# A graph network's pair loop: per-chunk target windows in steps of 64, and zero multiplies between the stages

## The chip, the core and the metric

The program runs on one core of one Trainium2 chip, in one launch. The metric is device time in microseconds, from the first to the last instruction and what the runtime puts around them; lower is better. A core has the engines TensorE (in the profile PE for its matmuls, PEld for its weight loads), VectorE (DVE), ScalarE (ACT), GpSimd (POOL) and SyncE (SP, here only DMA issues). [...]

## What is computed

One pass of four graph layers over 1024 nodes of 128 features, with 16384 edges sorted by target. Cut to what matters:

```python
# L0: a message per edge, summed by source node
m = concat([x[row], x[col]]); m = relu(relu(m @ Wm1 + bm1) @ Wm2 + bm2)
m_sum = segment_sum(m, row, 1024)
h = relu(relu(concat([x, m_sum, match(x)]) @ Wn1 + bn1) @ Wn2 + bn2)
# L1: three attention layers over the same edges, with a layer norm between them
# L2: mean over neighbours, then W;   L3: sum of neighbours weighted by edge_weight, then an MLP
```

Each layer is entered through a layer norm (ln0, ln1, ln4, ln5), and ln2 and ln3 stand between the attention layers. L1 needs how many edges lead from each node to each other, L2 whether there are any (with repeats kept up to a cap), L3 the sum of their weights. The kernel makes these as dense 1024 x 1024 matrices (counts and weights), while it computes L0's messages.

## The kernel before

**Sort.** The edges are sorted by the block of 128 nodes that their source lies in (`src >> 7`), stable, so within a block they keep the order of their targets. They are laid out in pairs of two chunks, 128 edges each (`PAIR` is 256); each block is padded to whole pairs. There are eight blocks and, with these inputs, 68 pairs. `dstf` holds each slot's target, `valid` says whether a slot is filled, one column a chunk.

**Pair loop.** For each block, a loop over its pairs `g` on four engines at once. TensorE multiplies one-hots: `OHc` (sources, with a rank cap) and `OHe` (sources times each of three parts of the edge's weight) against `OHd`, a chunk's one-hots of its targets, 1024 wide. The results add up in PSUM: banks 0 and 1 hold the block's 128 x 1024 counts, banks 2 and 3 the weights. Not all of the 1024 targets are gone over: `rngi` holds one packed number for each pair, the span, with the first block of 128 targets that the pair touches and the last one, and TensorE loads it into a register (L1230). A dynamic loop over the span (L1237), here called a pass, does two blocks of 128 targets at once, for both chunks: 16 matmuls.

The order of a pair on TensorE: ranks (L1176), load the span (L1230), source parts of the message of pair g + 2 (L1185), passes (L1242 counts, L1245 weights), message sums (L1251), ranks for the next pair (L1176), transposes and the two layers of the next pair's messages (L1163, L1170, L1171). Between engines it goes by semaphores:
- VectorE makes the next `OHd` (L928) when TensorE's first L1251 has signalled `counts_added`. Behind it come the rank products (L903), which signal `ranks_read`.
- TensorE's `ranks` of the pair wait for `ranks_read`, and all that follows on its sequencer stands behind that wait.
- ScalarE makes `OHe` (L546), `OHs32` (L548), and the activations (L557, L560). VectorE adds biases (L914) and messages (L888). GpSimd gathers table rows (L399) and turns sources into one-hots (L413).

**Setup of the spans.** VectorE marks for all chunks and all eight blocks of targets which slots lie in it (`inblk`, L826), TensorE sums the marks over the edges (L1195), and VectorE makes the first and last block of each pair from them (L849, L857, then the short operations from L861 to L876). The messages of the first two pairs (L860, L895) stand among these on VectorE.

**The normalisations.** For ln1 to ln5 VectorE makes mean and variance (L711, L712), ScalarE the root (L472, signals `ln_sd`), VectorE the scales and half of the rows (L725), ScalarE the others where it is shared. TensorE has nothing to do until the first rows are there. Its first work then is: ln1 eight transposes (L1075) and the rows of the attention (L1328); ln2 and ln3 transposes (L1321) and L1328; ln4 the means (L1436); ln5 the weighed sums (L1464).

The places that the change touches:

## Time and profile before

| | us |
|---|---|
| median of 3 runs | 999.43 |
| lowest, highest | 998.51, 1005.07 |
| the profiled execution, its own time | 995.34 |
| its span, first to last instruction | 993.5 |
| mean granted clock of TensorE | 0.962 |

The span is what the profile's rows add up to; 1.8 us lie around it. Rows give start and duration in microseconds from the span's start, or a count and nanoseconds of one. "Idle before" in brackets says how long an engine was idle ahead of a group and what released it; "issue" is time in which it waited for nothing that the profile shows. [...]

### The profile page before, as it was taken

How to read it: one execution, taken by the hardware profiler on the slowest of the kernel's cores; microseconds unless marked ns; L12 is line 12 of the kernel's file. 1: busy time of each engine (PE TensorE's matmuls, PEld its weight loads, DVE VectorE, ACT ScalarE, POOL GpSimd, SP SyncE). 2: the span in 40 equal slices, each digit the busy share in tenths (PEclk: the TensorE clock that was granted, in tenths of full speed). 3: DMA queues.
4: the chain of work that ended last, by engine and by line, in shares of the span. 5: the costliest groups of instructions: out<-in, count | busy, mean ns of one | idle time of the engine just before them, and what ended most of it. 6: DMA issues, size and time to landing. Idle time of an engine off the chain costs nothing.

```text
span 993.5 us, 18362 instructions
## 1 busy us (share of the span) xinstructions
PE 876.5 (88%) x5355; PEld 545.8 (55%) x5356; DVE 666.2 (67%) x1778; ACT 502.4 (51%) x1006; POOL 291.9 (29%) x424
## 2 busy tenths in 40 slices
PE   3999958999899999999999998689978996899668
PEld 1556736878787878787878745322232222322134
DVE  6399985666666666666666763577757784967650
ACT  6232104555555556555555564466645674566521
POOL 5030036545444545454544400011132110121000
PEclk9999987999999999999999999799979998999979
DMA  3020032111111111111112300000000000000300
GB/s 80 28 81 1 1 115 66 42 63 51 60 49 59 48 63 47 59 50 56 53 55 47 68 1 1 1 0 1 1 1 0 1 1 0 1 1 0 132 38 21
DMA packets 19144, 35.85 MB, mean 36 GB/s; under 512 B 5280, under 2 KB 11552, under 8 KB 18976
## 3 DMA queue, kind: packets, MB, share of 16 engines
q0 software_dynamic: 7104, 19.41, 6.9%
q1 hardware_dynamic: 12000, 15.95, 4.8%
q8 instruction: 20, 0.33, 0.1%
q14 instruction: 20, 0.16, 0.1%
HBM read 29.56 MB, written 5.79 MB: 36 GB/s over the span
## 4 chain that ended last, share of the span: by engine, by line
PE 75%; DVE 13%; ACT 6%; issue 3%; DMA 1%; POOL 1%; DVEq 0%; ACTq 0%; POOLq 0%
PE PS L1374 9%; PE PS L1251 7%; PE PS L1245 6%; PE PS L1170 5%; PE PS L1359 5%; PE PS L1171 5%; PE PS L1185 5%; PE PS L1120 4%; PE PS L1365 4%; PE PS L1328 3%; PE PS L1242 3%; PE PS L1292 3%; DVE OHd L986 3%; PE PS L1163 3%; PE PS L1176 2%
## 5 line engine op out<-in xcount | busy, mean ns | idle before, releaser
L399 POOL DMA_INDIRECT BT<-Qtab,gidx x148 | 149.9, 1013 | 96.3 <-DVE gidx L813 61.2
L546 ACT ACTIVATE OHe<-OHs,sew 128x128 bf16<-128x128 bf16 x408 | 126.6, 390 | 63.5 <-PE PS L1251 63.0
L986 DVE CUSTOM_DVE_ANT_0 OHd<-PS,n1T 128x1024 bf16<-128x1024 f32 x96 | 112.1, 1220 | 19.5 <-PE PS L1328 19.5
L413 POOL TENSOR_SCALAR KV<-BT,pid 128x256 bf16<-128x256 uint8 x74 | 69.9, 945 | 176.2 <-DVE MS L888 170.8
L557 ACT ACTIVATE m2s<-m2s 128x512 f32<-128x512 f32 x68 | 42.8, 630 | 108.4 <-DVE m2s L914 108.4
L928 DVE TENSOR_SCALAR OHd<-iotaN,dstf 128x1024 bf16<-128x1024 f16 x136 | 64.0, 509 | 37.6 <-PE PS L1251 37.5
L1170 PE MATMUL PS<-Wm,m1T 128*128 128x256 f32 x276 | 83.2, 383 | 0.0
L914 DVE TENSOR_TENSOR m2s<-PS,bm 128x512 f32<-128x512 f32 x68 | 47.0, 691 | 53.6 <-PE PS L1171 53.6
L1171 PE MATMUL PS<-Wm,m1T 128*128 128x256 f32 x276 | 82.6, 381 | 0.0
L452 POOL TENSOR_TENSOR zl<-AL,Sx 128x8 f32<-128x8 f32 x12 | 2.6, 216 | 265.1 <-DVE Sx L986 265.1
L1251 PE MATMUL PS<-OHs,m2s 128*128 128x128 f32 x544 | 79.9, 291 | 0.0
L1245 PE MATMUL PS<-OHd,OHe 128*128 x852 | 78.0, 225 | 0.0
L1120 PE MATMUL PS<-KV,m2s 128*128 128x288 f32 x256 | 72.6, 429 | 2.8 <-DVE KV L805 2.6
L1185 PE MATMUL PS<-SKT,KV 128*128 (+1 forms) x420 | 61.0, 282 | 14.5 <-issue 7.4
L888 DVE TENSOR_TENSOR MS<-PS,BT 128x512 f32<-128x512 f32 x68 | 47.0, 692 | 36.8 <-PE PS L1185 36.8
L1251 PEld LDWEIGHTS PS<-OHs,m2s 128*128 128x128 f32 x544 | 67.8, 196 | 6.4
L1242 PE MATMUL PS<-OHd,OHc 128*128 x284 | 64.2, 226 | 3.2 <-issue 0.6
L1365 PE MATMUL PS<-rowA,sel 128*128 128x512 bf16 x192 | 57.8, 382 | 10.4 <-ACT rowA L645 8.6
L805 DVE SCALAR_TENSOR_TENSOR KV<-iota,hi,carried 128x288 f32<-128x288 f32 x128 | 65.8, 514 | 0.0
L1120 PEld LDWEIGHTS PS<-KV,m2s 128*128 128x128 f32 x256 | 46.0, 195 | 27.3 <-DVE KV L805 14.5
L997 DVE SCALAR_TENSOR_TENSOR PS<-msum,s,BT 128x1024 f32<-128x1024 f32 x30 | 38.8, 1293 | 30.8 <-ACT Wn L654 24.1
L1245 PEld LDWEIGHTS PS<-OHd,OHe 128*128 128x128 bf16 x852 | 56.3, 100 | 4.3
(349 smaller groups left out, 1704.2 us busy)
## 6 DMA issues: line engine op xcount, KB each, us to landing
BT<-Wtab SPq DMA_DIRECT2D x1, 4096.0 KB, 12.8
BT<-Qtab,gidx POOLq DMA_INDIRECT x148, 2.8
BT<-Stab SPq DMA_DIRECT2D x1, 2048.0 KB, 10.2
Wtab<-H SPq DMA_DIRECT2D x4, 512.0 KB, 2.8
Wtab<-cs SPq DMA_DIRECT2D x4, 512.0 KB, 2.9
Qtab<-BT SPq DMA_DIRECT2D x1, 1024.0 KB, 4.5
Wn<-in_L_gnn_Wn SPq DMA_DIRECT2D x1, 1024.0 KB, 5.5
x<-in_x SPq DMA_DIRECT2D x1, 512.0 KB, 4.2
```

What stands on the lines that cost most here:

```text
L399: g.indirect_dma_start(out=G[:, p % SLOTS, k, :], out_offset=None, in_=Qtab, in_offset=bass.IndirectOffsetOnAxis(ap=gidx[:, p, k:k + 1], a ...
L546: a.activation(OHe[:, k, j, :], OHs[:, k, :], ACT.Copy, scale=sew[:, j, bass.ds(2 * g + k, 1)])
L986: v.tensor_tensor_reduce(junk[n % 2], bank(4, 2), mask[:, i, :], 1.0, 2 * FAR, ALU.subtract, ALU.max, Sx[:, i, hd:hd + 1]).then_inc(S("gat ...
L1120: t.matmul(bank(5)[:, 0:2 * NCH], OHlo[:, i % RING, :], KV[:, i % RING, :, :].rearrange("p k c -> p (k c)"), start=(i == 0), stop=(i == T ...
L1170: t.matmul(to, m1T[:, k, :], Wm2[:, 0, :], start=True, stop=False)
L1171: return t.matmul(to, m1T[:, 2 + k, :], Wm2[:, 1, :], start=False, stop=True)
L1185: last = t.matmul(bank(5)[:, k * F2:(k + 1) * F2], OHsT[:, slot, k * P:(k + 1) * P], Pp[:, blk, j, :], start=(j == 0), stop=(j == 2))
L1242: t.matmul(PS[:, bass.ds(at, P)], OHc[:, k, :], dst, start=False, stop=False, skip_group_check=True)
L1245: t.matmul(PS[:, bass.ds(at + 2 * BANK, P)], OHe[:, k, j, :], dst, start=False, stop=False, skip_group_check=True)
L1251: last = t.matmul(bank(4)[:, f * P:(f + 1) * P], m2s[:, k, f * P:(f + 1) * P], OHs32[:, k, :], start=False, stop=False, skip_group_check=True)
L1365: last = t.matmul(tile(hd, j)[:, half * BANK:(half + 1) * BANK], sel[:, half, :], rowA[:, hd % 2, :], start=False, stop=False, skip_group_ ...
L1374: last = t.matmul(bank(6 + hd % 2)[half * P // 2:half * P // 2 + C + 1, :], HX[:, j, hd, :], EC[n % 4][:, half * BANK:(half + 1) * BANK], ...
```

## The change

Each chunk gets a window of its own, 128 targets wide, that starts at a multiple of 64. The packed span holds the first unit of 64 targets of both chunks, how far the loop goes, and the block of the sources. A pass now does one window for each chunk: 8 matmuls. If a chunk touches three or more units, or starts in the last unit of a PSUM bank, both chunks of the pair start at an even unit and the pair takes as many passes as are needed. The ends of each chunk's targets come from transposing `dstf` and `rngp` and reducing over the edges, and the packed number is worked out in one row. Also, TensorE multiplies zeros (`steady`) while the normalisations run: a number of 128x512 multiplies ahead of the wait for `ln_sd`, some behind it, and five behind the transposes.

```diff
@@ -37,6 +37,8 @@
 FRAC = 1.0 / 1024.0
 FAR = -1e30
 BANK = 512
+UNITS = 15 << 6
+WFIRST, WCOUNT, WBLK = 1 << 6, 1 << 10, 1 << 14
 
 fp32, bf16, fp16 = mybir.dt.float32, mybir.dt.bfloat16, mybir.dt.float16
 i32, u32, i16, u8 = mybir.dt.int32, mybir.dt.uint32, mybir.dt.int16, mybir.dt.uint8
@@ -386,7 +387,7 @@
                 split(g.tensor_scalar(pblk[:, 1, :], iota[0:FEW, 0:NPAIR], pb[0:FEW, b:b + 1], None, ALU.is_ge))
                 split(g.tensor_tensor(pblk[:, 0, :], pblk[:, 0, :], pblk[:, 1, :], ALU.add))
             split(g.tensor_copy(pblki[:], pblk[:, 0, 1:2]))
-            g.tensor_scalar(pblk[:, 1, 0:NPAIR - 2], pblk[:, 0, 2:NPAIR], float(NB * NB), None, ALU.mult)
+            g.tensor_scalar(pblk[:, 1, 0:NPAIR - 2], pblk[:, 0, 2:NPAIR], float(WBLK), None, ALU.mult)
             g.memset(pblk[:, 1, NPAIR - 2:NPAIR], 0.0).then_inc(S("pair_blocks"), 1)
             eng.wait_ge(S("tables_stored"), 16)
             eng.wait_ge(S("indices_ready"), 1)
@@ -819,13 +819,9 @@
             link(v.tensor_copy(srcl[:], ssrc[:]))
             link(v.scalar_tensor_tensor(srcl[:], srcl[:], 1.0, valid[:], ALU.add, ALU.mult))
             v.tensor_scalar(srcl[:], srcl[:], -1.0, None, ALU.add).then_inc(S("sources_ready"), 1)
-            v.tensor_copy(paired(dstf), sdst)
-            link(v.tensor_scalar(paired(skey), sdst, 7, None, ALU.arith_shift_right))
-            link(v.tensor_copy(sew0[:], skey[:]))
-            link(v.scalar_tensor_tensor(rngp[:], sew0[:], 1.0, valid[:], ALU.add, ALU.mult))
-            v.tensor_tensor(inblk, rngp[:].unsqueeze(1).to_broadcast([P, NB, NCH]),
-                            iota[:, 1:NB + 1].unsqueeze(2).to_broadcast([P, NB, NCH]), ALU.is_equal)\
-                .then_inc(S("blocks_marked"), 1)
+            v.tensor_copy(paired(dstf), sdst).then_inc(S("dst_ready"), 1)
+            eng.wait_ge(S("dst_ready"), 1)
+            v.scalar_tensor_tensor(rngp[:], dstf[:], 0.0, valid[:], ALU.add, ALU.mult).then_inc(S("dst_ready"), 1)
 
             eng.wait_ge(S("sources_ready"), 1)
             for k in range(2):
@@ -833,6 +829,11 @@
             last.then_inc(S("src_onehots"), 1)
             for k in range(2):
                 v.tensor_scalar(OHd[:, k, 0:N], iotaN[:], dstf[:, k:k + 1], None, ALU.is_equal)
+
+            eng.wait_ge(S("dst_turned"), 1)
+            turned = bank(6).rearrange("p (m u e) -> p m u e", m=2, u=2)
+            v.tensor_reduce(ends[:, 0, :], turned[:, 0, :, :], AX.X, ALU.min).then_inc(S("ends_found"), 1)
+            v.tensor_reduce(ends[:, 1, :], turned[:, 1, :, :], AX.X, ALU.max).then_inc(S("ends_found"), 1)
 
             eng.wait_ge(S("sort_read"), 1)
             for k in range(3):
@@ -842,38 +843,38 @@
                     link(v.tensor_tensor(sewv[:], sewv[:], sew[:, k, :], ALU.subtract))
             v.tensor_copy(rank[:], sew[:, 0, 0:2]).then_inc(S("weights_split"), 1)
             made = bank(5).rearrange("p (k f) -> p k f", k=2)
-            eng.wait_ge(S("blocks_counted"), 1)
-            held = bank(6, 2)[0:FEW, :].rearrange("p (u n) -> p u n", u=2)[:, :, 0:NB // 2 * NPAIR]\
-                .rearrange("p u (b g) -> p u b g", g=NPAIR)
-            for i, rank_of in enumerate((falling[0:FEW, :], iota[0:FEW, 1:NB + 1])):
-                last = v.scalar_tensor_tensor(flags.rearrange("p (u b) g -> p u b g", u=2), held, 1.0,
-                                              rank_of.unsqueeze(2).to_broadcast([FEW, NB, NPAIR])
-                                              .rearrange("p (u b) g -> p u b g", u=2), ALU.min, ALU.mult)
-                if i:
-                    last.then_inc(S("blocks_read"), 1)
-                    eng.wait_ge(S("blocks_read"), 1)
-                else:
-                    link(last)
-                link(v.tensor_reduce(rngf[:, i, :], flags.rearrange("p b g -> p g b"), AX.X, ALU.max))
+            eng.wait_ge(S("ends_turned"), 1)
+            row = lambda m: unit_i[:, m, :]
+            link(v.tensor_copy(unit_i[:, 0:2, :], bank(7)[0:1, 0:2 * NCH].rearrange("p (m c) -> p m c", m=2)))
+            link(v.tensor_scalar(unit_i[:, 0:2, :], unit_i[:, 0:2, :], 6, None, ALU.arith_shift_right))
+            v.tensor_scalar(row(2), row(0), 7, None, ALU.bitwise_and)
+            link(v.tensor_scalar(row(3), row(0), 1, None, ALU.bitwise_and))
+            link(v.tensor_copy(unit, unit_i))
+            first, until, in8, odd = (unit[:, m, :].rearrange("p (g k) -> p g k", k=2) for m in range(4))
+            whole, count = apart[0:1, 0, :], apart[0:1, 1, :]
+            both = lambda t: t.unsqueeze(2).to_broadcast([1, NPAIR, 2])
+            spare = unit_i.bitcast(fp32)[:, 0, :].rearrange("p (g k) -> p g k", k=2)
+            link(v.tensor_tensor(until, until, first, ALU.max))
+            link(v.tensor_tensor(spare, until, first, ALU.subtract))
+            link(v.tensor_scalar(spare, spare, 2.0, None, ALU.is_ge))
+            link(v.scalar_tensor_tensor(in8, in8, 7.0, spare, ALU.is_equal, ALU.max))
+            link(v.tensor_tensor(whole, in8[:, :, 0], in8[:, :, 1], ALU.max))
+            link(v.tensor_tensor(odd, odd, both(whole), ALU.mult))
+            link(v.tensor_tensor(first, first, odd, ALU.subtract))
+            link(v.scalar_tensor_tensor(until, until, 2.0, first, ALU.add, ALU.subtract))
+            link(v.tensor_tensor(count, until[:, :, 0], until[:, :, 1], ALU.max))
             eng.wait_ge(S("gathered"), 1)
             eng.wait_ge(S("pparts_done"), 1)
             v.tensor_tensor(MS[:], made, G[:, 0, :, :], ALU.add).then_inc(S("msg_ready"), 1)
-            link(v.tensor_scalar(rngf[:, 1, :], rngf[:, 1, :], 1.0, -1.0, ALU.max, ALU.add))
-            link(v.tensor_scalar(rngf[:, 0, :], rngf[:, 0, :], -1.0, float(NB), ALU.mult, ALU.add))
-
-            link(v.tensor_tensor(rngf[:, 0, :], rngf[:, 0, :], rngf[:, 1, :], ALU.min))
-            link(v.tensor_tensor(rngf[:, 1, :], rngf[:, 1, :], rngf[:, 0, :], ALU.subtract))
-            link(v.tensor_scalar(rngf[:, 1, :], rngf[:, 1, :], 2.0, None, ALU.add))
-            link(v.tensor_copy(rngi[:], rngf[:, 1, :]))
-            link(v.tensor_scalar(rngi[:], rngi[:], 1, None, ALU.arith_shift_right))
-            link(v.tensor_copy(rngf[:, 1, :], rngi[:]))
-            link(v.tensor_scalar(nfrom[:], rngf[:, 1, :], -2.0, float(NB), ALU.mult, ALU.add))
-            link(v.tensor_tensor(nfrom[:], nfrom[:], rngf[:, 0, :], ALU.min))
-            link(v.tensor_scalar(rngf[:, 1, :], rngf[:, 1, :], 2.0, -1.0, ALU.mult, ALU.add))
-            link(v.tensor_tensor(rngf[:, 1, :], rngf[:, 1, :], nfrom[:], ALU.add))
+            link(v.tensor_copy(rngi[0:1, :], count))
+            link(v.tensor_scalar(rngi[0:1, :], rngi[0:1, :], 1, None, ALU.arith_shift_right))
+            link(v.tensor_copy(count, rngi[0:1, :]))
+            link(v.tensor_scalar(whole, count, -2.0, float(2 * NB), ALU.mult, ALU.add))
+            link(v.tensor_tensor(first, first, both(whole), ALU.min))
+            link(v.scalar_tensor_tensor(whole, first[:, :, 0], float(WFIRST), first[:, :, 1], ALU.mult, ALU.add))
             eng.wait_ge(S("pair_blocks"), 1)
-            link(v.tensor_tensor(rngf[:, 1, :], rngf[:, 1, :], pblk[:, 1, :], ALU.add))
-            v.scalar_tensor_tensor(rngi[:], nfrom[:], float(NB), rngf[:, 1, :], ALU.mult, ALU.add)\
+            link(v.tensor_tensor(whole, whole, pblk[0:1, 1, :], ALU.add))
+            v.scalar_tensor_tensor(rngi[0:1, :], count, float(WCOUNT), whole, ALU.mult, ALU.add)\
                 .then_inc(S("spans"), 1)
 
 
@@ -1068,6 +1069,11 @@
         @block.tensor
         def _(eng):
             t = nc.tensor
+
+            def steady(k, count):
+
+                for _ in range(count):
+                    t.matmul(bank(k), onesb[:], zb[:], start=True, stop=True)
 
             def transpose_nodes(src, banks):
 
@@ -1188,18 +1194,22 @@
                 last.then_inc(S("pparts_done"), 1)
 
             eng.wait_ge(S("sources_across"), 1)
-            eng.wait_ge(S("blocks_marked"), 1)
-            for u in range(2):
-                marks = inblk[:, u * NB // 2:(u + 1) * NB // 2, :].rearrange("p b (g k) -> p b g k", k=2)
-                for k in range(2):
-                    last = t.matmul(bank(6 + u)[0:FEW, 0:NB // 2 * NPAIR], onesb[:, 0:FEW], marks[:, :, :, k],
-                                    start=(k == 0), stop=(k == 1))
-            last.then_inc(S("blocks_counted"), 1)
+            eng.wait_ge(S("dst_ready"), 2)
+            t.matmul(bank(6), zeros[:, 0:P], zeros[:, 0:BANK], start=True, stop=True)
+            for m, column in enumerate((dstf, rngp)):
+                t.transpose(bank(6)[:, 2 * m * P:(2 * m + 1) * P], column[:, 0:P], ident[:])
+                last = t.transpose(bank(6)[0:NCH - P, (2 * m + 1) * P:(2 * m + 2) * P], column[:, P:NCH], ident[:])
+            last.then_inc(S("dst_turned"), 1)
+            eng.wait_ge(S("ends_found"), 2)
+            for m in range(2):
+                t.transpose(bank(7)[0:1, m * NCH:m * NCH + P], ends[:, m, 0:1], ident[:])
+                last = t.transpose(bank(7)[0:1, m * NCH + P:(m + 1) * NCH], ends[0:NCH - P, m, 1:2],
+                                   ident[0:NCH - P, 0:NCH - P])
+            last.then_inc(S("ends_turned"), 1)
 
             t.sem_inc(S("pair_done"), 1)
             t.sem_inc(S("ranks_done"), 1)
             t.sem_inc(S("counts_added"), 1)
-            eng.wait_ge(S("blocks_read"), 1)
             eng.wait_ge(S("P_parts"), 3)
             eng.wait_ge(S("turned_onehots"), 1)
             sources(0, 0)
@@ -1227,23 +1237,22 @@
                     eng.wait_ge(S("ranks_read"), g + 1)
                     ranks(((0, notbefb, 0), (0, onesb, 1), (1, notbefb, 1))).then_inc(S("ranks_added"), 1)
                     eng.wait_ge(S("spans"), 1)
-                    span = eng.value_load(rngi[0:1, bass.ds(g, 1)], min_val=1, max_val=NB * NB * NB - 1)
+                    span = eng.value_load(rngi[0:1, bass.ds(g, 1)], min_val=1, max_val=NB * WBLK - 1)
 
                     eng.wait_ge(S("turned_onehots"), g + 3)
-                    sources((g + 2) & (SLOTS - 1), (span >> 6) & (NB - 1))
+                    sources((g + 2) & (SLOTS - 1), (span >> 14) & (NB - 1))
 
                     eng.wait_ge(S("scaled_ready"), g + 1)
                     eng.wait_ge(S("counts_ready"), g + 1)
-                    with eng.Fori((span >> 3) & 7, (span & 7) + 1, 2) as d:
-                        for k in range(2):
-                            for i in range(2):
-                                at = d * P + i * P
-                                dst = OHd[:, k, bass.ds(at, P)]
-                                t.matmul(PS[:, bass.ds(at, P)], OHc[:, k, :], dst,
+                    first, second = span & UNITS, span << 6
+                    with eng.Fori(first, first + ((span >> 3) & (2 * UNITS)), P) as d:
+                        for k, at in enumerate((eng.snap(d & UNITS), eng.snap((second - first + d) & UNITS))):
+                            dst = OHd[:, k, bass.ds(at, P)]
+                            t.matmul(PS[:, bass.ds(at, P)], OHc[:, k, :], dst,
+                                     start=False, stop=False, skip_group_check=True)
+                            for j in range(3):
+                                t.matmul(PS[:, bass.ds(at + 2 * BANK, P)], OHe[:, k, j, :], dst,
                                          start=False, stop=False, skip_group_check=True)
-                                for j in range(3):
-                                    t.matmul(PS[:, bass.ds(at + 2 * BANK, P)], OHe[:, k, j, :], dst,
-                                             start=False, stop=False, skip_group_check=True)
 
                     eng.wait_ge(S("m2_ready"), g + 1)
                     for f in range(2):
@@ -1308,18 +1317,27 @@
                     last = t.transpose(bank(2 + i % 2).bitcast(bf16)[:, j * P:(j + 1) * P],
                                        CT[:, j, i * P:(i + 1) * P].bitcast(bf16), identb[:])
                 last.then_inc(S("maskT_done"), 1)
+            eng.wait_ge(S("bias_parts"), 1)
+            steady(4, 14)
+            eng.wait_ge(S("ln_sd"), 1)
+            steady(4, 12)
             eng.wait_ge(S("ln_low"), NB // 4)
             eng.wait_ge(S("ln_high"), NB // 2)
             transpose_nodes(h, 6).then_inc(S("ln1_Tp"), 1)
+            steady(4, 5)
             eng.wait_ge(S("ln1_hT"), 1)
             eng.wait_ge(S("mask_ready"), NB)
             eng.wait_ge(S("Wx_ready"), 2)
             for l in range(3):
                 if l:
+                    steady(0, 10)
+                    eng.wait_ge(S("ln_sd"), l + 1)
+                    steady(0, 5)
                     for b in range(NB):
                         eng.wait_ge(S(f"ln{l + 1}_h"), b + 1)
                         last = t.transpose(PS[:, 6 * BANK + b * P:6 * BANK + (b + 1) * P], h[:, b, 0:D], ident[:])
                     last.then_inc(S(f"ln{l + 1}_Tp"), 1)
+                    steady(0, 5)
                     eng.wait_ge(S(f"ln{l + 1}_hT"), 1)
 
                 def source_row(hd):
@@ -1429,6 +1447,9 @@
 
 
             eng.wait_ge(S("lone_added"), 1)
+            steady(0, 18)
+            eng.wait_ge(S("ln_sd"), 4)
+            steady(0, 15)
 
             def mean(k, g, half, first=False, last=False):
 
@@ -1453,6 +1474,9 @@
                                 start=True, stop=True)
                 if b % (NB // 2) == NB // 2 - 1:
                     last.then_inc(S("y2_done"), 1)
+            steady(0, 14)
+            eng.wait_ge(S("ln_sd"), 5)
+            steady(0, 9)
 
             def weighed(half, js):
 
```

Left out of the diff: the tiles `apart`, `ends`, `unit_i` and `unit` (views of the sort's buffers) take the place of `rngf`, `nfrom`, `inblk`, `flags` and `falling`, and the line that made `falling` is gone.

## Rows read from the trace of the kernel before

**Rows 1.** The page's first line.
```profile
span 993.5 us, 18362 instructions
```

**Rows 2.** The page's part 4, shares of the chain by line.
```profile
PE PS L1374 9%; PE PS L1251 7%; PE PS L1245 6%; PE PS L1170 5%; PE PS L1359 5%; PE PS L1171 5%; PE PS L1185 5%; PE PS L1120 4%; PE PS L1365 4%; PE PS L1328 3%; PE PS L1242 3%; PE PS L1292 3%; DVE OHd L986 3%; PE PS L1163 3%; PE PS L1176 2%
```

**Rows 3.** Register instructions of lines L1237, L1242, L1245, whole run: count, ns, first and last start.
```profile
L1237 PEldq ALU_OP  x349: 36/36/36, 159.4 to 563.6; - x175
L1237 PEldq FUSED_REGOPS  x71: 78/84/84, 159.8 to 562.6; - x71
...
L1242 PEldq FUSED_REGOPS  x213: 42/46/74, 160.1 to 563.3; - x107
...
L1245 PEldq FUSED_REGOPS  x142: 46/46/46, 160.0 to 563.0; - x142
```

**Rows 4.** The same for one pair, 372.5 to 378.2 us.
```profile
L1230 PEldq TENSOR_LOAD <-rngi x1: 309/309/309, 374.4 to 374.4; - x1
...
L1237 PEldq FUSED_REGOPS  x1: 78/78/78, 376.5 to 376.5; - x1
L1237 PEldq COMPARE_BRANCH  x1: 78/78/78, 377.6 to 377.6; - x1
```

**Rows 5.** Timeline of this pair: start, us, engine, line, operation, idle before.
```profile
372.24 1.15 PE L1251 MATMUL PS<-OHs,m2s 128*128 128x128 f32 x8
...
372.86 0.95 DVE L928 TENSOR_SCALAR OHd<-iotaN,dstf 128x1024 bf16<-128x1024 f16 x2 [0.44 <-PE PS L1251]
...
373.72 0.28 DVE L903 CUSTOM_DVE_ANT_0 prod<-OHs,PS 128x128 f32<-128x128 bf16 x1
...
376.62 0.10 PEld L1242 LDWEIGHTS PS<-OHd,OHc 128*128 128x128 f16 x1 [0.35 <-issue]
...
377.42 0.21 PEld L1245 LDWEIGHTS PS<-OHd,OHe 128*128 128x128 bf16 x3
...
377.75 0.48 PE L1251 MATMUL PS<-OHs,m2s 128*128 128x128 f32 x2
```

**Rows 6.** Timeline of L1251 in pairs 4, 5 and 6 of block 0.
```profile
184.19 1.15 PE L1251 MATMUL PS<-OHs,m2s 128*128 128x128 f32 x8
...
191.09 1.15 PE L1251 MATMUL PS<-OHs,m2s 128*128 128x128 f32 x8
...
196.51 1.15 PE L1251 MATMUL PS<-OHs,m2s 128*128 128x128 f32 x8
```

**Rows 7.** Windows: stretch, us, PE, PEld, DVE, ACT, POOL busy (x), PEclk, DMA.
```profile
258.43:261.84 3.41, 1.59 (x12) 0.71 (x9) 2.59 (x10) 1.21 (x5) 0.20 (x1) 1.00 0.49 177
466.64:470.05 3.41, 3.37 (x24) 3.04 (x25) 1.02 (x3) 1.01 (x2) 0.81 (x1) 0.50 0.00 0
729.47:739.71 10.24, 6.32 (x13) 3.31 (x14) 4.11 (x23) 3.57 (x5) 8.51 (x17) 0.50 0.01 2
831.87:835.28 3.41, 0.68 (x8) 0.57 (x8) 2.55 (x14) 1.19 (x1) 0.00 (x0) 1.00 0.00 0
941.09:951.33 10.24, 4.88 (x12) 1.76 (x13) 7.76 (x30) 4.25 (x9) 0.00 (x0) 0.50 0.50 202
964.99:971.81 6.82, 4.14 (x5) 1.85 (x6) 4.06 (x14) 1.86 (x5) 0.00 (x0) 0.50 0.01 2
```

**Rows 8.** Timeline at the first change of block after 255 us.
```profile
258.27 1.24 PE L1267 MATMUL PS<-hn 128*128 128x512 bf16 x5
```

**Rows 9.** Timeline of VectorE in the setup.
```profile
137.61 1.36 DVE L826 TENSOR_TENSOR cs<-rngp,iota 128x1152 bf16<-128x1152 f32 x1
...
148.03 0.17 DVE L861 TENSOR_SCALAR rngf<-rngf 32x72 f32<-32x72 f32 x1
...
151.64 0.67 DVE L895 TENSOR_TENSOR MS<-PS,BT 128x512 f32<-128x512 f32 x1
```

**Rows 10.** The chain in order of time: start, us, what.
```profile
630.07 3.79 PE PS L1328 x4
...
643.32 1.98 PE PS L1328 x4
```

10 lines of the change are left out of this document (4 added, 6 removed).

## The prediction

> **What bounds the kernel now.** I read the page first: the span is 993.5 us [rows 1], and the chain that ended last runs mostly over TensorE; the lines of the pair loop (L1251, L1245, L1170, L1171, L1185, L1242) lead it beside L1374 of the attention [rows 2]. That only says that the loop matters: its 68 pairs run from 159 to 564 us [rows 3].
>
> Then I read what one pair waits for. From one pair to the next L1251 starts 5.5 us later (372.24 to 377.75) [rows 5]. Follow it: the first L1251 matmul releases VectorE's destination one-hots (L928, at 372.86), behind them on the same engine stand the rank products (L903, 373.72, two of them), and these release TensorE's next step. TensorE's array is busy with the layers then, but its sequencer stood at the wait for the ranks, and goes on only now: it loads the packed span at 374.4, and reaches the branch that ends the pass over the targets at 377.6 [rows 4]. L1251 starts 0.1 us behind that branch. So the ring is 0.6 us (L1251 to L928), 0.9 and 0.5 us on VectorE, and 3.5 us in which the sequencer executes register instructions. The array's own work isn't in it: at 376.62 the first weight load of the counts comes after 0.35 us in which "issue" held it [rows 5].
>
> The test is a pair that goes over the targets twice. It does 16 more matmuls; three L1245 loads of 0.10 us each take 0.21 together, so they follow at under 0.06 us [rows 5], and 16 are 0.9 us of array time. Yet L1251 starts at 184.19, 191.09 and 196.51: the pair with two passes takes 6.90, its neighbour 5.42 [rows 6]. The price of a pass is 1.4 us, and it is fully exposed. In a pass the sequencer has from 376.5 (FUSED_REGOPS) to the branch at 377.6 one instruction for every 0.12 us: six FUSED_REGOPS, three ALU_OP, one branch [rows 3, 4]. The counts of rows 3 fit this: 71 passes in 68 pairs, 71 + 213 + 142 fused ones are six per pass, and 349 ALU_OP are 2 for each pair and 3 for each pass. Read against the code, a product and a sum of an address go together in a fused one, while a shift or a mask is an ALU_OP of its own.
>
> **Part 1, the pass over the targets.** Half of the matmuls of a pass go (16 to 8), 57 ns each. By the ring above that is worth nothing: the array waits for the sequencer already. What counts is instructions.
> - Ahead of the pass: a shift, a mask and a move become a mask and a move. One ALU_OP less, -0.10 us (an ALU_OP's 36 ns are shorter than the 46 of a fused one, so I put it a little under the mean of 0.12).
> - In a pass: before, 6 fused + 3 ALU + branch = 10. After, by reading the new code as the old one was lowered: a copy of d, its mask, span << 6, span & UNITS, subtract and add (one fused), the second mask: 6; two addresses for OHd and PS, and two for the weights' banks: 4 fused; the step, span >> 3, its mask, the sum with first: 4 ALU; the branch. That is 15. Nothing of it can be ahead of the first matmul's address but behind the wait, so all is on the ring. With 0.10 for an ALU_OP or copy and 0.12 for a fused one or a branch: 9 x 0.10 + 5 x 0.12 + 0.12 = 1.6; the same sum for before gives 1.14 where the trace has 1.24, so I take 1.7. Ends: 1.4 if the span's parts are computed once ahead of the pass, 1.9 if masks are computed twice. A pass goes up by 0.46 us (0.2 to 0.7).
> - More pairs need two passes. I computed both rules on the inputs of seed 0 (edges by block of 128 sources, in order of their targets, cut in pairs of 256). The old rule gives 71 passes, with the second ones in pair 5 of block 0 (the one of rows 6), pair 4 of block 2 and pair 5 of block 6. The new rule gives 84: 16 pairs with two. Such a pair is one with a chunk that touches three units of 64 targets, or starts in the last unit of a bank of 512 and goes on behind it.
> - Sum: 68 x (0.46 - 0.10) = 24.5; second passes after, 16 x (1.7 + 0.16 for the taken branch, the difference between 1.40 and 1.24) = 29.8; before, 3 x 1.40 = 4.2. **+50 us**, with ends 33 and 67.
>
> [...] The trace has the sequencer behind the ranks' wait until 374.4 and the array short of work at 376.62 [rows 4, 5]. [...]
>
> **Part 2, the clock inside the loop.** With 8 matmuls in 1.7 us, a pair with two passes has 3.5 us with little in it. At changes of block, stretches like this cost the clock before: the one from 466.64 ran at 0.50 behind such a gap, while 258.43 with 1.59 us busy kept 1.00 [rows 7]. Each fall costs up to half of that row's 3.4 busy us, about 1.3 after some is hidden in the sequencer's time. None to sixteen; I take three, **+4 us** (0 to 15).
>
> **Part 3, the setup of the spans.** Off VectorE go one 1152-wide comparison (L826, 1.36 us), the shift and cast ahead of it, two 576-wide products and reductions. On it come two reductions of 256 columns, and some 14 small operations on one row, at about 0.3 us each (L861 to L895 is 3.6 us for 12 links [rows 9]). Most of that lies beside TensorE's first source products, which wait for the sources' broadcast. Behind the first messages 8 links stand where 12 stood: 4 x 0.3 = **-1 us** on the path to L895. Ten transposes and one zero multiply are added on an idle TensorE. As VectorE could also be late for the first messages: -2 to +2.
>
> **Part 4, the zero multiplies.** Before each normalisation's matmuls the granted clock has fallen: 10.2 us at 0.50 from 729.47, from 941.09 and (two more such rows) from 623.65 and 835.28, and 6.8 us from 964.99 [rows 7]. [...]
> - ln1, ln2, ln3: four L1328 records take 3.79 us there and 1.98 later [rows 10]: -1.8 each. Transposes: ln1 has all eight behind one wait, -0.9; ln2 and ln3 are paced by VectorE, -0.25 each. Together -6.8.
> - ln4: 4.88 us of the means run at 0.50, -2.4. ln5: 4.14 us of the weighed sums, -2.1 [rows 7].
> Sum **-11.3 us** if the clock is held. Do zeros hold it? The stretch from 258.43 kept 1.00 with 1.59 us busy, of which 1.08 are the bank-clearing multiplies by zeros (L1267, until 259.51) [rows 8]; the one from 831.87 with 0.68 us of real ones lost it [rows 7]. So I count on them. [...] Ends: -12 and +8.
>
> **The sum.** 995.3 (the profiled execution, 993.5 span and 1.8 around it) + 50 + 4 - 1 - 11.3 = 1037. The median of the runs is 999.4, 4 us above the profiled one; I stay at the profiled one's scale plus a part of this, **1038 us**.
>
> **The rivals.**
> 1. The array is the bound, and register instructions are hidden (the end on the other side). Then passes cost by their matmuls: 71 x 16 - 84 x 8 = 464 fewer, x 0.057 = -26, with -11 and -1: 957 us. It decides if the sequencer's share of the ring falls below the array's work between L1251 and L1251, 5 us. Against it: the 1.4 us of the second pass where the array needs 0.9, and the "issue" ahead of L1242. 0.07.
> 2. The registers are cheaper than I count: shifts fused or hoisted, a pass at 1.25 to 1.3. Then 68 x (0.03 - 0.10) + 16 x 1.43 - 4.2 = +14, and 995 + 14 - 12 + 2 = 999: no change. For it: only the code tells me how it is lowered. Against it: every shift and mask before is an ALU_OP of its own. 0.10.
> 3. The zero multiplies don't hold the clock, and delay what they stand ahead of: 1037 + 11 + 5 = 1053. 0.08.
> 4. More falls of the clock in the loop, or a larger pass than 1.9: above 1058. 0.05.
> My forecast's own case has the remaining 0.70, and reaches from 1012 to 1058.
>
> **How the numbers follow.** Likeliest 1038. The range is the case's own, 1012 (a pass at 1.4 and all of part 4) to 1058 (a pass at 1.9, eight falls of the clock); rival 3 is inside it, rivals 1, 2 and 4 outside with 0.2 or a little more. A change under 1% can't be told from none here: faster 0.08 (rival 1), same 0.07 (most of rival 2), slower 0.85.
>
> **What would show it.** Right: 84 COMPARE_BRANCH in the pass, some 8 to 9 ALU_OP in each, a period near 5.8 us in a pair with one pass and 7.7 in one with two, the idle time before L1251's loads put to "issue"; 672 matmuls on the count lines; granted clock 1.00 in all five normalisations, and L1328 at 1.98 throughout. Wrong: a period below 5.4 (rival 1), or near 5.4 with cheap second passes (rival 2). If the clock at the normalisations is still 0.50, zeros don't count as work.

## The result and the profile after

The changed kernel takes 1026.35 us (median of 4 runs, 1022.97 to 1028.4) against 998.97 for the kernel before (4 runs, one more than in the table ahead, 998.51 to 1005.07): a ratio of 1.0256, 95% interval 1.0208 to 1.0305. It is 27 us slower where I forecast 39 over the median; the range 1012 to 1058 holds it. The profiled execution took 1026.91.

The page's first line answers [rows 1]: the span grew by 31.6 us while 433 instructions fell away.

```profile
span 1025.1 us, 17929 instructions
```

The chain by line answers [rows 2] (L1260 is the old L1251, L1176/L1177 the layers, L1191 the source products, L1251 and L1254 the counts and weights, which were L1242 and L1245).

```profile
PE PS L1392 8%; PE PS L1260 8%; PE PS L1176 5%; PE PS L1177 5%; PE PS L1377 5%; PE PS L1191 5%; PE PS L1383 4%; PE PS L1126 4%; PE PS L1254 4%; PE PS L1251 3%; PE PS L1169 3%; PE PS L1301 3%; DVE OHd L987 3%; PE PS L1182 2%; PE PS L1346 2%
```

The weights' share fell from 6% to 4% and that of the message sums (L1260) rose from 7% to 8%. The chain shows the array, so it can't say what the sequencer did. For that, the instructions of the pass by line, whole run, as in [rows 3] (PEldq marks register instructions and branches of TensorE's sequencer; durations min/median/max in ns, first and last start in us):

```profile
L1248 PEldq ALU_OP  x236: 32/32/43, 159.7 to 602.8; - x118
L1248 PEldq MOVE  x152: 29/29/38, 159.8 to 601.6; - x152
L1248 PEldq FUSED_REGOPS  x84: 66/73/73, 161.0 to 602.6; - x84
L1248 PEldq COMPARE_BRANCH  x84: 77/83/241, 161.3 to 602.9; - x84
...
L1251 PEldq FUSED_REGOPS  x252: 60/74/129, 160.1 to 602.3; - x126
L1251 PEldq ALU_OP  x168: 32/32/42, 160.0 to 602.2; - x168
...
L1254 PE MATMUL PS<-OHd,OHe x504: 219/219/314, 160.5 to 602.7; 128*128 x168
L1254 PEldq FUSED_REGOPS  x168: 46/46/46, 160.2 to 602.4; - x168
```

84 branches are 84 passes, as computed. Divided by them: a move (152 less one for each of 68 pairs), four ALU_OP (236 - 68 and 168), six fused ones (84 + 252 + 168) and the branch, twelve instructions in a pass. I had forecast fifteen.

One pair with two passes, as in [rows 4]. From the second move (534.6) to the second branch (536.0) the sequencer takes 1.4 us start to start; before it was 1.1 from 376.5 to 377.6 [rows 4].

```profile
L1240 PEldq TENSOR_LOAD <-rngi x1: 316/316/316, 531.0 to 531.0; - x1
...
L1248 PEldq MOVE  x3: 29/29/29, 532.9 to 534.6; - x3
...
L1248 PEldq COMPARE_BRANCH  x2: 83/152/222, 534.3 to 536.0; - x2
```

The timeline around it, as in [rows 5] and [rows 6]:

```profile
528.86 1.15 PE L1260 MATMUL PS<-OHs,m2s 128*128 128x128 f32 x8 [0.19 <-issue]
...
533.27 0.10 PEld L1251 LDWEIGHTS PS<-OHd,OHc 128*128 128x128 f16 x1 [0.39 <-issue]
...
534.92 0.10 PEld L1251 LDWEIGHTS PS<-OHd,OHc 128*128 128x128 f16 x1 [0.80 <-issue]
...
536.12 1.15 PE L1260 MATMUL PS<-OHs,m2s 128*128 128x128 f32 x8 [0.19 <-issue]
...
541.74 1.15 PE L1260 MATMUL PS<-OHs,m2s 128*128 128x128 f32 x8 [0.19 <-issue]
```

With two passes 7.26 us, with one 5.62. Between the last load of one window and the first of the next pass the loads wait 0.80 us, for nothing that the profile shows ("issue"), while the sequencer executes the register instructions of the pass. L1260, which before followed the counts directly, now waits 0.19 for it too. Over the loop the pair of one pass at full clock goes from 5.48 to 5.60 us (medians), that of two from 6.90 to 7.24.

The windows, as in [rows 7] (the number behind POOL's is PEclk, the granted clock of TensorE as a share of full speed):

```profile
188.78:192.19 3.41, 3.41 (x18) 3.17 (x17) 1.97 (x9) 2.17 (x7) 1.03 (x1) 0.50 0.27 77
687.12:693.95 6.83, 6.83 (x18) 1.82 (x17) 4.72 (x7) 3.63 (x4) 0.00 (x0) 0.75 0.01 2
765.63:772.45 6.82, 6.82 (x60) 3.15 (x58) 6.11 (x31) 3.15 (x5) 4.49 (x10) 0.50 0.00 0
772.45:782.69 10.24, 10.02 (x47) 5.97 (x46) 5.57 (x9) 4.59 (x10) 4.34 (x9) 1.00 0.01 2
972.97:983.21 10.24, 9.22 (x47) 4.08 (x47) 8.27 (x34) 4.59 (x9) 0.00 (x0) 1.00 0.88 353
```

The first row is one of eleven stretches in the loop (one of double length) at the lower level, 0.50, where before had three; they are called falls from here on. At ln1, and from 772.45 on through the later normalisations, the clock stays at 1.00. Two falls stand between: one in the first attention layer (687.12), where before had none, and one at ln2 (765.63 to 772.45), with the zero multiplies themselves running in it. The timeline of TensorE at ln2 and, behind the dots, at ln3 (L1076 are the zero multiplies, L1338 the transposes, which were L1321):

```profile
766.71 6.22 PE L1076 MATMUL PS<-zb,onesb 128*128 128x512 bf16 x15
772.77 1.04 PE L1338 MATMUL PS<-ident,h 128*128 128x128 f32 x8
...
873.65 1.25 PE L1076 MATMUL PS<-zb,onesb 128*128 128x512 bf16 x5 [1.30 <-ACT sd L473]
875.08 2.12 PE L1338 MATMUL PS<-ident,h 128*128 128x128 f32 x8 [0.17 <-DVE h L726]
```

At ln2 fifteen zero multiplies take 6.22 us (0.41 each, against 0.25 at ln3), and the transposes come behind them. From VectorE's first statistics (L712, 765.83) they start 6.9 us later; at ln3 it is 4.3 us (870.83 to 875.08), and they wait there only for VectorE. The chain in order of time, as in [rows 10]:

```profile
668.32 2.00 PE PS L1346 x4
...
775.10 2.00 PE PS L1346 x4
...
878.50 2.00 PE PS L1346 x4
```

The four matmuls behind a normalisation take 2.00 us each time instead of 3.79. From the second of these rows to the third it is 103.40 us (before 105.36: 735.79 to 841.15), but from the first to the second 106.78 (before 105.72: 630.07 to 735.79): the two falls there ate the gain. The one at 687.12 took 1.7 us (from the second group of L1346 to the third, 679.78 to 701.29, 21.5 us, where before took 19.8); at ln2 the rows of L1346 come 9.3 us behind L712's start, where before took 8.1.

**Where the time went.** The L1260 row of the whole run bounds the loop: first start 161.5, last 603.9, so 442.4 us; before, L1251 ran from 161.7 to 564.7, 403.0 us. The loop lost 39.4 us. Ahead of it 0.2 us were gained, behind it 7.6: 1025.1 - 603.9 = 421.2 against 993.5 - 564.7 = 428.8. 39.4 - 0.2 - 7.6 = 31.6, the difference of the spans.

### The profile page after: what moved, and what is told of

Same layout as the page of the kernel before. It is cut to its first block, busy times and chain, and to the rows that moved or that the text cites. A ratio compares the mean times of both kernels' runs of the same rounds, so it can differ in the third digit from the quotient of the medians.

```text
span 1025.1 us, 17929 instructions
## 1 busy us (share of the span) xinstructions
PE 908.8 (89%) x5023; PEld 543.7 (53%) x5024; DVE 664.2 (65%) x1780; ACT 502.1 (49%) x1006; POOL 293.0 (29%) x424
## 4 chain that ended last, share of the span: by engine, by line
PE 74%; DVE 13%; ACT 6%; issue 5%; DVEq 0%; DMA 0%; ACTq 0%
PE PS L1392 8%; PE PS L1260 8%; PE PS L1176 5%; PE PS L1177 5%; PE PS L1377 5%; PE PS L1191 5%; PE PS L1383 4%; PE PS L1126 4%; PE PS L1254 4%; PE PS L1251 3%; PE PS L1169 3%; PE PS L1301 3%; DVE OHd L987 3%; PE PS L1182 2%; PE PS L1346 2%
## 5 line engine op out<-in xcount | busy, mean ns | idle before, releaser
L400 POOL DMA_INDIRECT BT<-Qtab,gidx x148 | 150.5, 1017 | 96.3 <-DVE gidx L813 61.1
L558 ACT ACTIVATE m2s<-m2s 128x512 f32<-128x512 f32 x68 | 42.8, 630 | 126.7 <-DVE m2s L915 119.1
L1260 PE MATMUL PS<-OHs,m2s 128*128 128x128 f32 x544 | 87.4, 310 | 10.6 <-issue 6.9
L1176 PE MATMUL PS<-Wm,m1T 128*128 128x256 f32 x276 | 86.1, 395 | 0.0
L1260 PEld LDWEIGHTS PS<-OHs,m2s 128*128 128x128 f32 x544 | 73.9, 211 | 22.3 <-issue 18.8
L1177 PE MATMUL PS<-Wm,m1T 128*128 128x256 f32 x276 | 83.6, 385 | 0.0
L1191 PE MATMUL PS<-SKT,KV 128*128 (+1 forms) x420 | 61.4, 283 | 12.7 <-issue 8.3
L1177 PEld LDWEIGHTS PS<-Wm,m1T 128*128 128x128 f32 x276 | 54.3, 197 | 8.1
L1254 PE MATMUL PS<-OHd,OHe 128*128 x504 | 58.1, 228 | 0.0
L1251 PE MATMUL PS<-OHd,OHc 128*128 x168 | 38.9, 232 | 20.9 <-issue 9.9
## 6 DMA issues: line engine op xcount, KB each, us to landing
BT<-Stab SPq DMA_DIRECT2D x1, 2048.0 KB, 10.2
```

What stands on the lines that cost most here:

```text
L400: g.indirect_dma_start(out=G[:, p % SLOTS, k, :], out_offset=None, in_=Qtab, in_offset=bass.IndirectOffsetOnAxis(ap=gidx[:, p, k:k + 1], a ...
L1176: t.matmul(to, m1T[:, k, :], Wm2[:, 0, :], start=True, stop=False)
L1177: return t.matmul(to, m1T[:, 2 + k, :], Wm2[:, 1, :], start=False, stop=True)
L1191: last = t.matmul(bank(5)[:, k * F2:(k + 1) * F2], OHsT[:, slot, k * P:(k + 1) * P], Pp[:, blk, j, :], start=(j == 0), stop=(j == 2))
L1254: t.matmul(PS[:, bass.ds(at + 2 * BANK, P)], OHe[:, k, j, :], dst, start=False, stop=False, skip_group_check=True)
L1260: last = t.matmul(bank(4)[:, f * P:(f + 1) * P], m2s[:, k, f * P:(f + 1) * P], OHs32[:, k, :], start=False, stop=False, skip_group_check=True)
```

## The experiments

Ratios are to the kernel before, in runs on the same chip (its median there was 996.1 to 996.3). "Loop" is the stretch from the first to the last start of the message sums, m2s times one-hots (L1251 before, 403.0 us; L1260 after, 442.4).

**e1, the windows alone.** The changed kernel without the zero multiplies and the waits that they brought.

```diff
-            eng.wait_ge(S("bias_parts"), 1)
-            steady(4, 14)
...
-            steady(0, 9)
```

> The change without its zero multiplies: windows and spans as changed, nothing between the stages. My theory (the pass is bound by the sequencer's register instructions, and the zeros hold the clock at the normalisations): the pair loop is as long as in the changed kernel, 442 us against 403 before, and the clock is at 0.50 again before the five stages, so about 11 us above the changed kernel: 1036 to 1039 us. Rival (the zero multiplies buy nothing, or cost, as they stand ahead of the real work): at or below the changed kernel, 1020 to 1027 us.

1034.3 us (1030.37 to 1040.09), ratio 1.0401 (1.0365 to 1.0436). Loop 437.5, outside it 591.1 us of the span of 1028.6, against 582.7 in the changed kernel and 590.5 before: the zero multiplies gave 8.4 us there. The windows alone cost 38 us. The time lies 2 us under the expected 1036 to 1039, and the loop 4.9 us under the changed kernel's, though both run the same instructions in it. Nearly all of this (4.4 us) lies in the pairs in which the clock had fallen in one of the two.

**e2, the zero multiplies alone.** The kernel before with all of them.

```diff
+            def steady(k, count):
+                for _ in range(count):
+                    t.matmul(bank(k), onesb[:], zb[:], start=True, stop=True)
...
```

> The kernel before with the zero multiplies alone. My theory: the loop stays at 403 us, the clock stays at 1.00 in the five normalisations, 9 to 11 us less: 988 to 990 us. Rival (zeros don't count, and delay): 999 to 1005 us.

987.06 us (985.08 to 989.0), ratio 0.991 (0.9889 to 0.993): -9.1 us. Loop 402.7, unchanged; outside it 581.8, 8.7 less. Granted clock 0.983 over the run, against 0.953 to 0.962 before. The gain is within the 9 to 11 us expected, but the clock isn't at 1.00 in all five normalisations: at ln2 it is at 0.50 from 725.5 to 732.3 us, as in the changed kernel. So the change is a loss of 38 and a gain of 9 in one.

**e3, eight matmuls less, the same registers.** Left out are the second and third part of the weights.

```diff
-                                for j in range(3):
+                                for j in range(1):
```

> The kernel before with one of the three parts of the edge weights in a pass instead of three: 8 matmuls a pass as in the change, every register instruction kept. It leaves out the second and third part of the weights. Sequencer theory: the period of a pair stays at 5.4 to 5.5 us and the loop at 401 to 403 us; a second pass still costs 1.3 to 1.4 us; within 3 us of the kernel before. Array theory (the removed matmuls are worth 0.057 us each): 71 x 8 x 0.057 = 32 us less, 967 us.

995.07 us (10 runs), ratio 0.9997 (0.9984 to 1.001). The timeline of L1251:

```profile
340.39 1.15 PE L1251 MATMUL PS<-OHs,m2s 128*128 128x128 f32 x8 [0.17 <-issue]
345.86 1.15 PE L1251 MATMUL PS<-OHs,m2s 128*128 128x128 f32 x8 [0.16 <-issue]
```

5.47 us, as before. 568 fewer matmuls in the run are worth nothing; in their place stands idle time that "issue" ends. Rival 1, by which this run would take 967 us, fell here.

**e4, the load moved.** The kernel before with the packed span read ahead of the wait for the ranks.

```diff
+                    eng.wait_ge(S("spans"), 1)
+                    span = eng.value_load(rngi[0:1, bass.ds(g, 1)], ...)
                     eng.wait_ge(S("ranks_read"), g + 1)
                     ranks(((0, notbefb, 0), (0, onesb, 1), (1, notbefb, 1))).then_inc(S("ranks_added"), 1)
-                    eng.wait_ge(S("spans"), 1)
-                    span = eng.value_load(rngi[0:1, bass.ds(g, 1)], ...)
```

> The kernel before with the packed span loaded and its bounds tested ahead of the wait for the ranks, where the sequencer stands idle for 0.9 us of each pair. Not a matmul less. Sequencer theory: 0.7 us of register work leaves the ring of a pair; the array's own work of a pair, about 5.0 us, then is next: period 5.0 us or a little under, 25 to 32 us less, 967 to 975 us. Array theory: nothing changes, 997 to 1001 us.

958.28 us (957.21 to 959.15), ratio 0.9621 (0.9605 to 0.9637), loop 364.7. The timeline of the weight loads of one pair:

```profile
350.40 0.59 PEld L1185 LDWEIGHTS PS<-SKT,KV 128*128 x6
351.00 0.10 PEld L1242 LDWEIGHTS PS<-OHd,OHc 128*128 128x128 f16 x1
351.11 0.21 PEld L1245 LDWEIGHTS PS<-OHd,OHe 128*128 128x128 bf16 x3
351.27 0.10 PEld L1242 LDWEIGHTS PS<-OHd,OHc 128*128 128x128 f16 x1
```

And of its message sums and the next pair's:

```profile
352.00 1.11 PE L1251 MATMUL PS<-OHs,m2s 128*128 128x128 f32 x8
357.00 1.11 PE L1251 MATMUL PS<-OHs,m2s 128*128 128x128 f32 x8
```

No "issue" stands ahead of the counts in this pair any more (0.35 in [rows 5]), the loads follow at 0.06 us, and the pair takes 5.00. The load of the span starts at 348.2, 2.1 us ahead of the ranks' matmuls (350.28); before it was 1.2 us (374.4 and 375.57). No work was removed: only the order on the sequencer was changed. That is the ring of the prediction, shown. The clock falls of the loop are gone too. The pair came out as expected, but the time lies 9 us under the 967 to 975: 0.48 us in each of 68 pairs are 33 us, and the rest of the loop's 38 is the three falls and the pairs at a change of block (8.42 us instead of 9.13 for the first of them).

**e5, the change with the early load.** The same edit in the changed kernel.

> The changed kernel with one edit: the word of the windows is loaded ahead of the wait for ranks_read, as in e4. Sequencer theory: with the load out of the stretch ahead of the counts the array is continuous, as in e4 (there 5.05 us a pair of one pass, the counts' eight loads 0.056 us apart), so the eight matmuls less of a pass count for the first time: up to 8 x 0.056 = 0.45 us; about 0.15 to 0.3 us of it is left, because the pass's twelve register instructions (1.44 us) come out just behind. 68 pairs give -10 to -25 us against e4, the 13 added second passes of about 1.5 us give +20, the setup -1, the zero multiplies -9: 958 -> 938 to 955 us, about 948; the pair of one pass 4.65 to 4.9 us. Rival (the sequencer stays the bound in the counts, whatever is loaded early): pairs of one pass stay at 5.1 us or more and the time is 965 to 980.

974.06 us (971.17 to 977.28), ratio 0.9779 (0.9748 to 0.981), loop 391.0. It misses the expected 938 to 955 and fits the rival's number, but not its reason. The timeline of the message sums:

```profile
347.34 1.15 PE L1260 MATMUL PS<-OHs,m2s 128*128 128x128 f32 x8 [0.18 <-ACT m2s L558]
352.30 1.15 PE L1260 MATMUL PS<-OHs,m2s 128*128 128x128 f32 x8 [0.18 <-ACT m2s L558]
```

The pair takes 4.96 here, and what ends last is neither array nor sequencer but ScalarE's part of the second layer's result (L558); it ends L1260's wait 29 times in the run. The median pair of one pass is 4.99, and many of the others take about 5.1. A third bound stands 0.05 us under e4's period, so the halved matmuls had nowhere to go; the 16 second passes (median pair 6.62) stay.

**e6, registers hoisted.** e5, with slot, block, first window, end and distance put into registers ahead of the wait for the ranks.

```diff
+                    slot = kept((g + 2) & (SLOTS - 1), 0, SLOTS - 1)
+                    blk = kept((span >> 14) & (NB - 1), 0, NB - 1)
+                    first = kept(span & UNITS, 0, 2 * UNITS)
+                    until = kept(first + ((span >> 3) & (2 * UNITS)), 0, 5 * UNITS)
+                    apart = kept(((span << 6) & UNITS) + (UNITS + P // 2) - first, 0, 4 * UNITS)
...
```

> e5, and the registers that don't depend on the pass (slot, source block, first window, end of the loop, distance of the two windows) are worked out behind the load, ahead of the wait for ranks_read; a pass keeps 10 of its 12 register instructions, and two to three fall away between the last wait and the first count. Sequencer theory: the counts wait less for their addresses; pairs of one pass fall to the array's 5.05 - 0.45 = 4.6 us, a second pass costs 1.3 instead of 1.5 to 1.65 us: 5 to 12 us below e5, about 940 us. Rival (the array or VectorE's chain is the bound once the load is early): within 2 us of e5. Second rival (the sequencer has no room ahead of ranks_read either, so what is put there comes back): slower than e5 by up to 5 us.

982.65 us (981.62 to 983.07), ratio 0.9866 (0.9849 to 0.9882): 8.6 us slower than e5, loop 398.7. The second rival had the direction right, and the loss is larger than its 5 us. The timeline of the message sums, with the first load of the counts between them:

```profile
344.55 1.15 PE L1270 MATMUL PS<-OHs,m2s 128*128 128x128 f32 x8
...
348.98 0.10 PEld L1261 LDWEIGHTS PS<-OHd,OHc 128*128 128x128 f16 x1 [0.40 <-issue]
...
349.87 1.15 PE L1270 MATMUL PS<-OHs,m2s 128*128 128x128 f32 x8
```

The hoisted instructions, by line, whole run:

```profile
L1242 PEldq ALU_OP  x408: 32/32/42, 155.4 to 556.9; - x136
L1242 PEldq FUSED_REGOPS  x272: 57/62/148, 155.6 to 557.0; - x136
L1242 PEldq MOVE  x68: 29/29/35, 155.8 to 556.3; - x68
```

Eleven instructions a pair (748 in 68) go in ahead of the ranks, some 1.2 us at 0.11 each, and the pair goes to 5.32. The free place behind the load was already filled by e5: from the load (345.8) to the branch of the pass (349.7) one register instruction now follows the other without a wait that can be seen, and the counts wait 0.40 us for "issue" again. So here hoisting found no time left in which the sequencer waits; with a pass of ten instructions instead of twelve it still lost 8.6 us.

**e7, both gains.** The kernel before with e4's move and e2's multiplies.

> The kernel before with two edits: the zero multiplies of the change (all four places) and the early load of e4. If the two gains add: 958.3 x 0.991, 949 to 950 us. If the clock that the zero multiplies hold was in part already held by the shorter, continuous loop: 952 to 957.

947.51 us (946.64 to 950.57), ratio 0.9525 (0.9502 to 0.9547). The gains add: 10.8 us below e4, or 0.0096 in the ratios, where e2 had 0.009.

**e8, e7 with slot, block and end hoisted.**

```diff
+                    slot = kept((g + 2) & (SLOTS - 1), 0, SLOTS - 1)
+                    blk = kept((span >> 6) & (NB - 1), 0, NB - 1)
+                    until = kept((span & 7) + 1, 1, NB)
```

> e7, and slot, source block and end of the loop are worked out ahead of the wait for ranks_read, as in e6; a pass has 9 register instructions instead of 10. Array theory of the early kernels (the array is continuous in e4's loop): nothing is left for registers to hide, the time is within 2 us of e7, about 949; only the three second passes gain. Sequencer theory pushed further: 3 to 8 us below e7.

945.85 us (945.02 to 946.15), ratio 0.9495 (0.948 to 0.9511): 1.7 below e7, inside the "within 2 us" of the array theory. It is the fastest version, 5.1% under the kernel before; its step against e7 is small beside the spread of e7's own runs (946.64 to 950.57).

**e9, the array's work put back.** The changed kernel with eight more multiplies by zeros in a pass, without registers.

```diff
+                            for _ in range(4):
+                                t.matmul(PS[:, 0:P], zeros[:, 0:P], zeros[:, 0:P],
+                                         start=False, stop=False, skip_group_check=True)
```

> The changed kernel with eight more matmuls in each pass, with zeros for both operands, added to the counts' memory without any register, so that a pass has the array work of before (16 matmuls) and the registers of the change. Theory: the 11 to 12 clock falls in the changed loop, against 3, come from the array's shorter work; with the work put back they go, and with them 6 to 9 us, while the eight matmuls cost nothing, because the sequencer is the bound (e3): 1017 to 1021 us, the pair of one pass at 5.60 us as in the change. Rival (the falls come from the longer waits for registers, whatever the array does in a pass): 11 or 12 falls stay and the time is 1025 to 1028. Second rival (the matmuls do cost, 8 x 0.056 us in 84 passes): 1045 or more.

1023.4 us (1019.73 to 1023.86), ratio 1.0268 (1.0245 to 1.0291), loop 437.0. The added multiplies, by line:

```profile
L1257 PE MATMUL PS<-hn x672: 219/219/315, 161.4 to 598.6; 128*128 128x128 bf16 x168
```

In pairs of one and of two passes the added matmuls cost nothing (5.60 and 7.25 us), as e3 had it the other way round. Only a pair at a change of block takes about 0.5 us more (9.96 against e1's 9.48, the first of them). The time lies between the expected ranges, 1017 to 1021 and 1025 to 1028, and far from the 1045 of the second rival. Of the falls six stay in the loop, each at the first pair of a block. But e1, without padding, had seven (one double) in an almost equal loop of 437.5. So the padding is not shown to remove any, and the array's shorter work is not shown as the cause of falls: the profiled execution of the changed kernel simply had more (eleven) than that of e1, whose loop runs the same instructions.

**e10, one pass for each pair.** The changed kernel; left out are the counts of the second passes.

```diff
-                    with eng.Fori(first, first + ((span >> 3) & (2 * UNITS)), P) as d:
+                    with eng.Fori(first, first + ((span >> 3) & P), P) as d:
```

> The changed kernel with the loop's end cut so that each of the 68 pairs takes one pass; left out are the counts of the second passes of 16 pairs. Instructions per pass and pair are the same. Theory: the 16 second passes cost 7.24 - 5.60 = 1.64 us each, 26 us in all, and one or two clock falls behind them: 997 to 1001 us. Rival (a second pass is in part slack that the next pair gives back): 1005 to 1012.

993.93 us (989.41 to 996.27, 10 runs), ratio 0.9975 (0.9958 to 0.9992), loop 408.3. The passes, by line:

```profile
L1248 PEldq COMPARE_BRANCH  x68: 77/78/105, 160.1 to 567.6; - x68
```

Against e1's loop 29.2 us less, 1.82 for each of 16 second passes, 3 us more than 16 x 1.64: 1.4 of the 3 lie in e1's third and fourth pairs (6.59 and 5.97 us against 5.60 and 5.60 here), in which only e1's clock had fallen. The time is 3 us under the expected 997 to 1001; the rival's 1005 to 1012 is out. Without the second passes the change would be a draw, with the zero multiplies' 9 us in it.

**e11, four more register instructions.** The kernel before, with masks that change no value; 14 instructions in a pass instead of 10.

```diff
+                        ats = [eng.snap((d * P + i * P) & (NB * P - P)) for i in range(2)]
```

> The kernel before with four more register instructions in a pass (14 instead of 10), masks that change no value; passes, matmuls and setup are those of before. Theory: a register instruction of a pass costs about 0.10 us of the pair, less what lay idle on the sequencer: after had two more and 0.12 us more, so four give 0.24 to 0.40 us in each of 68 pairs, the pair at 5.75 to 5.85 instead of 5.48: 1013 to 1024 us. Rival (the queue behind the array covers them): 996 to 999.

1018.55 us (1018.31 to 1020.18), ratio 1.0234 (1.0217 to 1.0251), loop 426.5. The timeline of L1251:

```profile
346.39 1.15 PE L1251 MATMUL PS<-OHs,m2s 128*128 128x128 f32 x8
352.14 1.15 PE L1251 MATMUL PS<-OHs,m2s 128*128 128x128 f32 x8
```

With the passes, matmuls and setup of before, register instructions alone make it 22 us slower, as expected: the pair 5.75 (median 5.76, +0.29), that of two passes 7.57 instead of 6.90. That is the mechanism of the change in a pure form. Its profiled loop has six falls where before had three, with the array's work of a pass unchanged.

**e12, e4 with eight matmuls less** (second and third part of the weights left out, as in e3).

> e4 (the kernel before, with the load of the spans ahead of the wait for ranks_read) with eight matmuls less in each pass, as in e3; left out are the second and third part of the weights. e3 showed that these matmuls cost nothing before (0.9997). Theory: with the early load the array is the bound (5.05 us a pair, no gap at the counts), so now they cost: 0.15 to 0.35 us of a pair until the sequencer is the bound again: 936 to 949 us against 958. Rival (the sequencer is still the bound after e4): 957 to 960.

958.8 us (957.84 to 959.68), ratio 0.9626 (0.961 to 0.9642): the rival's number; loop 366.5 against e4's 364.7. The timeline of L1251:

```profile
336.18 1.16 PE L1251 MATMUL PS<-OHs,m2s 128*128 128x128 f32 x8 [0.17 <-ACT m2s L557]
341.12 1.16 PE L1251 MATMUL PS<-OHs,m2s 128*128 128x128 f32 x8 [0.17 <-ACT m2s L557]
```

The pair falls from 5.00 to 4.94, where ScalarE's result ends the wait, as in e5 (56 times in the run, in e4 never). The 3 us that this gives over the loop come back: its clock fell three times, in e4's loop never, and the three pairs in which it did take 3.9 us more. So the rival's reason, the sequencer, is not what the trace shows: in e4 two limits, the array (5.00) and ScalarE's m2s (4.94), lie 0.06 us apart.

## Why the prediction was right, and which of its terms were off

1. **The ring over the sequencer: right.** e3 and e9 show that matmuls of a pass are free in either direction (pairs of 5.47 us with eight less against 5.48, of 5.60 with eight more as without), e11 that registers are not (0.29 us for four), e4 that 38 us hang on where one load stands. The profile's durations are about half of what these instructions take: the twelve of the second pass in the changed kernel's pair (from 534.6) are drawn with 0.66 us together, an ALU_OP with 32 ns, and take 1.4 us start to start. The array's share of a pass was read right. The L1245 weight loads of before have a median of 98 ns over the whole run (852 of them, 95 to 152), so three in 0.21 us follow at 0.056, and 16 are 0.9 us by estimate; in e4, where nothing holds the counts, the 16 take 0.89, from the first (351.11) to L1251 (352.00).
2. **Rival 1, the array as the bound (957 us): not so in this loop.** With eight matmuls less in a pass e3 stays at 0.9997. e4 comes out at 958, by another way, and that the two numbers agree is chance. Its load of the span starts 2.1 us ahead of the ranks' matmuls instead of 1.2, while the message sums and the layers keep the array busy (346.96 to 350.45), and is hidden there. Before, it stood behind the wait for the ranks, and the counts waited 0.35 us for "issue".
3. **The size of a pass: too large.** "That is 15" was the step that failed; the trace has 12. I had taken the mask of the first window to be worked out in each pass, and every shift to be an ALU_OP of its own; as the counts read, the first window is computed once ahead of the loop, the left shift goes into a fused one as a product, and the right shift into the one with the step. Taking 1.7 us instead of the sum's 1.6 enlarged it again. The pair of one pass rose by 0.12 us, not 0.36 (to 5.60, and that of two passes to 7.24, where I had named 5.8 and 7.7 as signs): 68 x 0.12 = 8 us instead of 24.5. Two instructions more at 0.11 less the 0.10 ahead give just this. Rival 2 had the reason half right, that shifts are fused or hoisted; its price of a pass, 1.25 to 1.3 us, was too low for twelve instructions. My low end was also added up wrongly: a pass of 1.4 us gives 68 x 0.06 + 16 x 1.56 - 4.2 = 25, not 33, and the measured 30 lies above it.
4. **The number of passes: right, their price nearly.** 84, 16 pairs with two; the second costs 7.24 - 5.60 = 1.64, not 1.86. 16 x 1.64 - 3 x 1.42 = 22 us instead of 25.6. This term, not the first, is most of the loss.
5. **The clock in the loop: too small.** The rest of the loop's 39.4 us is 39.4 - 8 - 22 = 9. I put it down to the falls, eleven (twelve by length) instead of three in the profiled execution: e1's loop, with four less by length, was 4.9 us shorter, and nine more at 1.2 us each are 11, near that. I had 4, with ends 0 and 15: the price of a fall was right (1.3), their number too small. The number is no constant: seven in e1 and six in e10.
6. **The setup:** -0.2 us on the path instead of -1, inside its ends.
7. **The zero multiplies: right in kind, smaller.** -7.6 us instead of -11.3, and -8.7 alone in e2. From the rows behind the second normalisation to those behind the third (L1346 at full clock at the one, the transposes at the other) the gain was as forecast, -1.96 us against -2.05. The end gave 94.0 us from the last L1346 on (931.08) where it was 98.0 from 895.53, -4.0 of -4.5. Missing are 3.1 us between the first two: 1.7 by the fall at 687.12, and 1.4 at ln2, where the clock had fallen at 765.63, just ahead of the zeros, so that they ran at 0.50 (0.41 us each instead of 0.25) and delayed the transposes. This I had in the end of +8 and in rival 3's delay of 5 us, both as all or nothing; no run shows either of these terms. The runs showed 1.4 us at one normalisation of five, so the sign "1.00 in all five" failed there.

30 + 9 - 0.2 - 7.6 = 31 us between the profiled executions, where the forecast's terms gave 42: 20 too much in the passes, against 5 too little in the clock, 4 too much gain from the zeros and 1 from the setup. That these went against each other helped the number; the mechanism doesn't rest on it. The medians differ by 27 only: the kernel before's was 4 us above its profiled execution, and was 996 in all later comparisons.

**Open:** why the same loop has eleven falls in one execution and seven in another; no run fixed the clock by itself. Their number moves from execution to execution: of the changed kernel's four, the one with a mean granted clock of 0.970 took 1022.97 us and the one with 0.961 took 1028.4. So six falls in e11 against three before, each from one execution, don't show that register instructions bring them. What the rest of e10's 3 us is stays open too.

## What to carry to other kernels

When an engine's loop takes its addresses from loaded values, count sequencer instructions (here about 0.11 us each, while a taken branch alone is drawn with 0.22), not matmuls, and look where they stand against the waits. Moving one load ahead of a wait gave 38 us; halving the matmuls behind it gave nothing before (e3, 0.9997) and nothing after (e12, 958.8 against 958.28 us). A change that halves the work of a step but repeats the step in more cases must be priced by the step's fixed cost: 13 more passes cost 22 us, while the 464 fewer matmuls had nothing to give (568 fewer gave nothing in e3).
